# Experts' rows read back, added and normalized inside the next stage; the feed-forward's token mix put into its weights; the output stored by chunk

## The reference, cut to what matters

```
x = x + 0.5*moe0(LN(x)); x = x + heads0(LN(x)); x = x + 0.5*moe0(LN(x))     # ffn0a, mix0, ffn0b
x = x + 0.5*swiglu(LN(x)); x = x + attn1(LN(x)); x = x + 0.5*swiglu(LN(x))  # ffn1a, attn1, ffn1b
x = x + 0.5*moe2(LN(x)); x = x + decay2(LN(x)); x = x + 0.5*moe2(LN(x))     # ffn2a, decay2, ffn2b
x = x + 0.5*ffn3(LN(x)); x = x + timemix(LN(x)); x = x + 0.5*ffn3(LN(x))    # ffn3a, mix3, ffn3b

swiglu(x) = (silu(x @ wg.T) * (x @ wu.T)) @ wd.T                    # hidden 384
moe(x)    = sum over the 2 best of 8 experts of gate * expert(x)    # hidden 512
ffn3(x):  old = x one token earlier in its sequence (0 at its start)
          xr = mu_r*x + (1-mu_r)*old;  xk = mu_k*x + (1-mu_k)*old
          return sigmoid(xr @ Wr.T) * (relu(xk @ Wk.T)**2 @ Wv.T)
```

## Time and profile before

| | us |
|---|---|
| median of 3 runs (lowest, highest) | 3032.1 (3024.76, 3034.76) |
| profiled execution, its own time | 3018.49 |
| its span in the trace | 3016.6 |
| PE, DVE, ACT, POOL busy in the span | 2305.8, 2076.6, 1463.9, 913.7 |

### The profile page before, as it was taken

One profiled execution on the slowest core, in us unless ns is written; L12 is line 12 of the kernel. 1 busy time (PEld: TensorE's weight loads), 2 busy tenths in 40 slices (PEclk: granted clock), 3 DMA queues, 4 the chain that ended last, 5 costly groups with the idle time before them and its releaser, 6 DMA issues. The chain is left out here.

```text
span 3016.6 us, 45161 instructions
## 1 busy us (share of the span) xinstructions
PE 2305.8 (76%) x13720; PEld 1429.0 (47%) x13720; DVE 2076.6 (69%) x5273; ACT 1463.9 (49%) x3122; POOL 913.7 (30%) x960
## 2 busy tenths in 40 slices
PE   3497788859677799899899977679586965677774
PEld 3487577749644122222222224479465964222223
DVE  4466788746634799999999934556585666577775
ACT  2265312126534388888888862256433653223222
POOL 5544245534413200100100003644265441132230
PEclk9999799869889699999999988789796987899997
DMA  4122100012201300000000000122211230000000
GB/s 152 47 63 74 35 8 18 17 37 66 86 28 40 129 20 20 17 20 18 19 19 17 12 19 25 35 59 64 71 33 51 64 96 27 0 0 0 0 0 28
DMA packets 111194, 115.74 MB, mean 38 GB/s; under 512 B 21904, under 2 KB 94192, under 8 KB 110192
## 3 DMA queue, kind: packets, MB, share of 16 engines
q1 hardware_dynamic: 92512, 76.38, 8.6%
q0 software_dynamic: 17408, 35.95, 3.6%
q10 hardware_dynamic: 1040, 0.53, 0.1%
HBM read 67.55 MB, written 44.83 MB: 37 GB/s over the span
## 5 line engine op out<-in xcount | busy, mean ns | idle before, releaser
L1775 DVE TENSOR_REDUCE attn_mx<-bank 128x1 f32<-128x512 f32 x1024 | 640.7, 682 | 61.1 <-PE bank L1554 52.7
L1676 ACT ACTIVATE attn_pT<-bank 128x512 f32<-128x512 f32 x1024 | 539.9, 604 | 126.4 <-PE bank L1569 125.8
L1554 PE MATMUL bank<-attn_K,attn_Q 48*128 48x512 bf16 x1024 | 336.6, 397 | 49.8 <-DVE attn_mx L1775 29.2
L1569 PE MATMUL bank<-attn_Q,attn_K 51*128 51x512 bf16 x1024 | 331.4, 387 | 2.5 <-ACT attn_pT L1676 1.6
L1582 PE MATMUL bank<-attn_pT,attn_vb 128*32 128x512 f32 x2048 | 275.9, 610 | 19.9 <-ACT attn_pT L1676 11.8
L1735 POOL TENSOR_TENSOR attn_m_rem<-attn_m_rem,attn_m_parts 8x128 f32<-8x128 f32 x128 | 53.3, 416 | 678.6 <-ACT attn_m_parts L1689 678.6
L1554 PEld LDWEIGHTS bank<-attn_K,attn_Q 48*128 48x128 bf16 x1024 | 71.8, 94 | 375.1 <-DVE attn_mx L1775 324.3
L2436 POOL TENSOR_TENSOR mix_rS<-mix_rT,mix_S 128x512 f32<-128x512 f32 x64 | 81.5, 1277 | 265.3 <-ACT mix_gT L2417 204.9
L943 PE MATMUL bank<-mix_prod_qk,ident 128*128 128x256 f32 x512 | 118.5, 385 | 0.0
L943 PEld LDWEIGHTS bank<-mix_prod_qk,ident 128*128 128x128 f32 x512 | 98.9, 195 | 23.8 <-issue 11.2
L2370 PE MATMUL bank<-mix_rS,mix_sel 128*128 128x512 f32 x128 | 74.8, 672 | 42.4 <-POOL mix_rS L2436 42.4
(11 more groups left out here) (619 smaller groups left out, 5864.4 us busy)
## 6 DMA issues: line engine op xcount, KB each, us to landing
w<-in_L_w SPq DMA_DIRECT2D x4, 2048.0 KB, 10.4
ffn0a_x_ring<-xs_rows SPq DMA_DIRECT2D x72, 65.0 KB, 1.8
ffn0b_x_ring<-xs_rows SPq DMA_DIRECT2D x72, 65.0 KB, 1.8
ffn2a_x_ring<-xs_rows SPq DMA_DIRECT2D x72, 65.0 KB, 1.8
...
```

The source lines that it names most:

```text
L1554: nc.tensor.matmul(a_bank[n % 3][:], slot(net.Q, h, 0, KROWS)[:, qt * P:(qt + 1) * P], slot(net.K, h, 0, KROWS)[:, hf * CH:(hf + 1) * CH], ...
L1569: nc.tensor.matmul(s_bank[n % 3][:], slot(net.K, h, 0, KROWS + MROWS)[:, kt * P:(kt + 1) * P], slot(net.Q, h, 0, KROWS + MROWS)[:, hf * CH ...
L1676: nc.scalar.activation(pT[:, kt % RING, hf * CH:(hf + 1) * CH], s_bank[(n * HPB + hf) % 3][:], ACT.Exp, scale=HD ** -0.5).then_inc(exp_rea ...
L1775: nc.vector.tensor_reduce(mx[:, h % 2, qt, hf:hf + 1], a_bank[n % 3][:], AX.X, ALU.max).then_inc(a_used, 1)
```

## The change

Four edits.

1. The tail leaves the experts' stages ffn0b and ffn2b (`dest` None: no read back, no norm). The stages behind, ffn1a and ffn3a, get a `Returned` object, `front`: SP's `fetch` into three buffers, POOL's `pair_sum` (adds the two rows), DVE's `combine` (one add into x), `stats`, `apply`, ACT's `spread`, PE's `turn` into bank 5, ACT's `keep` into `src`. It works on chunk c+2 while the stage is at chunk c. Its norm keeps its small tiles twice (`deep`). ffn0a and ffn2a keep their tail.
2. The feed-forward's mix leaves DVE: `fold` (DVE, once a stage) makes `k_now = mu*W` and `k_old = W - k_now`, the same for r, and PE accumulates two products, one with the chunk and one with the chunk from one token earlier. Where a sequence begins, the first tile of the gates uses a copy, `first_tile_late`, with a column of zeros that POOL writes.
3. Keys, gates and values get two banks each, and the round is staggered: `keys(c)`, `values(c-1)`, back norm of c-2.
4. ffn3b's SP stores a chunk of x as soon as it is whole; `store_stage` is gone.

SP's issues also move: in ffn3a three fetches stand ahead of the 16 weight loads and five behind them; in ffn1a the loads of cos and sin stand behind all fetches.

```diff
 class Norm:  # mean_var, shift, var_eps, rstd and xn get a leading index c % self.depth (2 if deep, else 1)
...
-            need(dve, self.rstd_ready, c)
+            need(dve, self.rstd_ready, c - self.depth + 1)
...
+class Returned:
+    BUFS = 3
...
+    def fetch(self, sp, c):
+        rows = self.net.y_rows[0:Y_SPARE, :].rearrange("(t p k) d -> p t (k d)", p=P, k=TOPK)
+        need(sp, self.combined, c - self.BUFS + 1)
+        sp.dma_start(self.y[:, c % self.BUFS, :].rearrange("p (t r) -> p t r", t=TPC),
+                     self.norm.view3(rows, c)).then_inc(self.fetched[c % self.BUFS], 16)
+    def pair_sum(self, pool, c):
+        y = self.pairs(c)
+        pool.wait_ge(self.fetched[c % self.BUFS], 16 * (c // self.BUFS + 1))
+        self.nc.gpsimd.tensor_tensor(y[:, 0], y[:, 0], y[:, 1], ALU.add).then_inc(self.summed, 1)
+    def combine(self, dve, c):
+        x = self.norm.view(self.net.x, c)
+        dve.wait_ge(self.summed, c + 1)
+        self.nc.vector.tensor_tensor(x, x, self.pairs(c)[:, 0], ALU.add).then_inc(self.combined, 1)
...
 def swiglu_stage(...):  # PE
                     gate_up(c + 1, 0)
                     gate_up(c + 1, 1)
+                if front and c + 2 < NCH:
+                    front.norm.turn(pe, c + 2)
...
                 silu(c, 1)
+                if front and c + 1 < NCH:
+                    front.norm.keep(act, c + 1, spread=False)
                 silu(c, 2)
                 if depth > 0:
                     norm.keep(act, c - 1)
+                if front and c + 2 < NCH:
+                    front.norm.spread(act, c + 2)
...
 def rwkv_ffn_stage(nc, net, tag, src, dest, weights, out=None):
+                for c in range(NCH):                       # SP, ffn3a
+                    front.fetch(sp, c)
+                    if c == 2:
+                        weights.load(sp)
...
+                    sp.wait_ge(x_whole, c + 1)             # SP, ffn3b
+                    sp.dma_start(dst[:, c * TPC:(c + 1) * TPC], x[:, c * TPC:(c + 1) * TPC]).then_inc(stored, 16)
...
+            def keys(c):
+                nc.tensor.matmul(k_bank[c % 2][:], k_now[:], src[:, c * CH:(c + 1) * CH], start=True, stop=False,
+                                 skip_group_check=True)
+                nc.tensor.matmul(k_bank[c % 2][:, skip:CH], k_old[:], src[:, c * CH - 1 + skip:(c + 1) * CH - 1],
+                                 start=False, stop=True, skip_group_check=True).then_inc(k_ready, 1)
...
+                    nc.tensor.matmul(r_out, src[:, at:at + P], r_now[:], start=True, stop=False)
+                    ins = nc.tensor.matmul(r_out, before, r_old[:], start=False, stop=True)
...
+            for c in range(-1, NCH + 2):                   # PE
+                if front and c + 1 < NCH:
+                    front.norm.turn(pe, c + 1)
+                if 0 <= c < NCH:
+                    keys(c)
+                if 0 <= c - 1 < NCH:
+                    values(c - 1)
+                if norm and 0 <= c - 2:
+                    norm.turn(pe, c - 2)
...
+            for c in range(-2, NCH + 2):                   # ACT
+                if front and 0 <= c + 1 < NCH:
+                    front.norm.keep(act, c + 1, spread=False)
+                if c == -1:
+                    first_tile_late(0)
+                if norm and 0 <= c - 2:
+                    norm.spread(act, c - 2)
+                if 0 <= c < NCH:
+                    relu(c)
+                    sigmoid(c)
+                    if c + 1 < NCH and (c + 1) % HPB == 0:
+                        first_tile_late(c + 1)
+                if norm and 0 <= c - 2:
+                    norm.keep(act, c - 2, spread=False)
+                if front and c + 2 < NCH:
+                    front.norm.spread(act, c + 2)
```

More of the change, by code:

```diff
@@ L779, in _ @@
                     down(i, first[i % GROUP])
-            for c in range(NCH):
+            for c in range(NCH if norm else 0):
                 norm.turn(pe, c)
@@ L1187, in _ @@
                 powers.load(sp)
+            for c in range(NCH if front else 0):
+                front.fetch(sp, c)
             for t, w in preload:
@@ L1230, in tail @@
                     norm.count(pe)
+            if front:
+                front.norm.turn(pe, 0)
             gate_up(0, 0)
             gate_up(0, 1)
+            if front:
+                front.norm.turn(pe, 1)
             deep_rounds(body, tail)
@@ L1247, in body @@
                     norm.keep(act, c - 1)
+                if front and c + 2 < NCH:
+                    front.norm.spread(act, c + 2)
+            if front:
+                front.norm.spread(act, 0)
+                front.norm.keep(act, 0, spread=False)
+                front.norm.spread(act, 1)
             deep_rounds(body, lambda c: norm.all_act(act, c))
@@ L1292, in body @@
                     norm.place(dve, c - 2)
+                if coming:
+                    front.norm.apply(dve, c + 2)
                 add(c)
@@ L1313, in tail @@
                     norm.table(dve)
+            for c in range(2 if front else 0):
+                front.combine(dve, c)
+                front.stats(dve, c)
+                front.norm.apply(dve, c)
             deep_rounds(body, tail)
@@ L2213, in add @@
-                dve.wait_ge(x_whole, c + 1)
-            def body(c, b, hf):
-                mix(c, hf)
-                if not is_first(c):
-                    add(c - 1, 1 - hf)
+                nc.vector.scalar_tensor_tensor(x, gated[:, c % 2, :], 0.5, x, ALU.mult, ALU.add).then_inc(x_whole, 1)
+            fold()
+            for c in range(-2, NCH + 2):
+                if front and c + 2 < NCH:
+                    front.combine(dve, c + 2)
+                if norm and 0 <= c - 2:
+                    norm.apply(dve, c - 2)
+                if front and c + 2 < NCH:
+                    front.stats(dve, c + 2)
+                if 0 <= c < NCH:
+                    square(c)
+                if front and c + 2 < NCH:
+                    front.norm.apply(dve, c + 2)
+                if 0 <= c - 1 < NCH:
+                    add(c - 1)
```

263 lines of the change are left out of this document (152 added, 111 removed).

## The result

After the change the kernel takes 2977.7 us, median of 4 runs (2974.7 to 2982.3); before, 3032.6 (3024.8 to 3034.8). The ratio is 0.9827, 95% interval 0.9812 to 0.9842: 54.9 us less, where 50.8 were forecast. The profiled execution took 2976.2, span 2974.1.

What follows compares the result with a forecast made beforehand. No engine was taken as full: loops over DVE, PE and ACT and the serial tails of ffn0b and ffn2b bound the kernel. Savings 18.5+21.2+11.1 = 50.8 us take 3032.1 to 2981; 8 in 10 from 2968 to 3002.

Steps and rivals of the forecast that it cites:

- offset: Whole kernel: the profiled execution was 13.6 us faster than the median of the runs, and this difference was kept.
- First term: ffn0b and ffn1a: tail goes, 21.5 us gained at the start, 3.0 lost to extra transposes; 18.5 saved.
- Second term: ffn2b and ffn3a: tail goes, first key product 18.4 us after the fetch, end at 2557.7; 21.2 us saved.
- sum 1 holds the add: Start of ffn3a's front: POOL's pair sum of chunk 1 delays DVE's combining add of chunk 0 by 1.1 us.
- The locks of rounds 2 to 4: ffn3a: back shift collides with POOL's pair sum, both excluding each other; 1.1 us more in each of these rounds.
- Fetch 3 behind 16 weight loads: SP's queue in ffn3a: costed at nothing, covered by 6 us; 0 to 3 us if the loads delayed it more.
- Third term: ffn3b: mix folded into weights, PE sets rounds of 4.45 us, chunks stored at once; 11.1 us saved, stores 5.7.
- More locks: Rival, ffn3a and ffn1a: pair sums also hold an add or square; 10 us more, 2991; chance 0.19 with clock rival.
- Fewer: Rival: the shift wins every race and ramp losses vanish, 2974, or 2971 with overlapped spreads; more saved, chance 0.13.
- the rival's 0.77: Rival, ffn3a: clock stays at 0.77, 9 us more, 2990; at 0.6, 3006; chance 0.19 together with locks.
- The case that both feed-forward stages run at the lower clock: Rival "slower", ffn3a and ffn3b: PE held at lower clock, 3053 us; decides from about 0.57; chance 0.03.
- three signs of being wrong: ffn3a keys over 10 us apart, either stage's first add waiting over 8 for landing, column-shifted products over 0.9.

Runs made afterwards that it cites:

- e10: The kernel before, with only the stores of the output by chunk inside ffn3b added; ratio 0.9968 to the kernel before.

## Why the prediction was right

**Sum and offset.** 50.8 forecast, 54.9 measured. The sum was made against a profiled execution 13.6 us quicker than the median, and the offset was kept. That was right: e10, whose code is that of before up to ffn3b, has its first fetch behind ffn0b 4 us later and that behind ffn2b 8.6 later, so 8.6 of the 13.6 lay in stages that no edit touches; and the profile of after lies 1.5 from its median. The time, 2977.7, is inside the forecast's own range, 2973 to 2990. That the total came within about 4 us owes something to luck: the terms missed by -1.1, +3.5 and +0.6, and the steps inside them by more, as follows.

**First term, 18.5: 17.4 measured.** The first gate product came 13.8 us behind the fetch (14.0 forecast), with the pair sum at 1.25 (1.1) and the shift's lock at 1.07 (1.1); the second round started 22.3 earlier (21.5). A round at full clock grew by 0.35 (0.50). What was missing is the clock: I let ffn1a keep its level, and one or two more `down` of 1.63 us extra fell to the lower one. The Trainium skill (TensorE: Matmul & The Clock Gate, Why this matters for your kernels) warns of idle gaps between bursts of matmuls. The rows agree that idle time brings the lower clock, but a shorter wait than the page names, 2.28 a round, came with it here in some rounds, in before already.

**Second term, 21.2: 24.7 measured, the largest miss.** The first key product came at 16.6, not 18.4: the step "sum 1 holds the add" failed. The add of chunk 0 won the race by 0.2 us and held the sum (1.60), which did not matter; that step had been costed at 1.1, and two powers taken at 1.41 each were 1.02 and 1.04 there. The stage's end was forecast 95.2 behind the fetch; the mark, which lies 0.7 to 0.9 behind that end, stands at 92.2 in the mean. The locks of rounds 2 to 4 were there, three shifts of 1.22 to 1.23, but they and the low clock were added up, and they overlap: a full round is 7.7 to 7.9, about 9 with the lock, or 9.4 at low clock with or without it. Fetch 3 behind 16 weight loads was hidden, as costed: its pair sum starts 15.3 behind the first fetch, the first square 20.9.

**Third term, 11.1: 11.7 measured.** Key products stand 4.4 apart (4.45), PE has no gap. The stores were undersized, 7.1 for 5.7: from the last issue to the end I kept 4.7, and in after and e10, where the last store is issued by itself, it is 3.2. The rest is 4.6 for 5.4. The fold had its 1.1 in the sum, and the first key product stands where it was forecast, 2.5 behind mix3's last turn (2.6). The loss lies behind it. In after, the second key product follows the first by 6.2, 2.6 more than keys and gates take at full clock, where 1.8 was costed; and the last add starts 1.3 behind the last values, where 0.7 was.

**Rivals.** "More locks" did not come: no add or square on the path was held; one combining add of ffn1a took 1.65 beside a pair sum, between two `down` 11.3 apart, where others at full clock are 11.2. "Fewer" did not come either: six shifts took 1.22 to 1.23. Two numbers of the rivals were wrong without bearing on the forecast: 10 of the 16 pair sums stand in the stages' loops, not 12, and at a clock of 0.57 the two losses of 27 make 54, not 51. The clock of ffn3a stayed above the rival's 0.77 in the steady part, 0.88, though under my 0.95. The case that both feed-forward stages run at the lower clock was excluded by ffn3b's 0.98. None of the three signs of being wrong appeared: key products of ffn3a are at most 9.4 apart, the first pair sum starts 4.3 to 4.4 behind the fetch, and the two products of the keys, with the operand as it is and shifted by a column, take 0.86 each in ffn3b.

**Open.** Why four rounds in one execution and three in the next fall to the lower clock was not settled. The fold and the staggered round were not tested apart. That POOL's power takes 1.38 to 1.40 with DVE's add or square under way was seen, not tested by itself.
